# When the hidden product of a shared expert frees its banks, and where its steps stand among the routing

## What is computed

```python
    def swiglu(x):
        g = x[..., ::2]
        l = x[..., 1::2]
        g = jnp.minimum(g, LIMIT)
        l = jnp.clip(l, -LIMIT, LIMIT)
        return g * jax.nn.sigmoid(ALPHA * g) * (l + 1.0)
    xt = x.reshape(-1, d)
    scores = jax.nn.softmax(xt @ gate_w.T, axis=-1)
    _, idx = jax.lax.top_k(scores + gate_b, TOPK)
    ...
    h = swiglu((xt @ ew1 + eb1) * (xt @ ew3 + eb3))
    return (acc + ce[:, None] * (h @ ew2 + eb2), None)
    ...
    shared = swiglu((xt @ sw1 + sb1) * (xt @ sw3 + sb3)) @ sw2 + sb2
    return (routed + shared).reshape(b, s, d)
```

## Time and profile before

| | |
|---|---|
| time, median of 3 runs | 969.93 us (966.49 to 972.44) |
| time of the profiled execution | 972.44 us |
| its span | 970.7 us |
| PE busy | 889.3 us (92%) |
| DVE busy | 644.4 us (66%) |
| ACT busy | 529.9 us (55%) |
| POOL busy | 387.0 us (40%) |

### The profile page before, as it was taken

The page is one execution under the profiler, slowest core; times in us unless marked ns, Lnnn a source line. Parts: engine busy times, 40 slices in busy tenths (PEclk is TensorE's granted clock), DMA queues, the critical chain, the costliest instruction groups (busy, mean ns, idle before and its releaser), DMA issues.

```text
span 970.7 us, 15074 instructions
## 1 busy us (share of the span) xinstructions
PE 889.3 (92%) x4286; PEld 620.1 (64%) x4287; DVE 644.4 (66%) x1309; ACT 529.9 (55%) x843; POOL 387.0 (40%) x321
## 2 busy tenths in 40 slices
PE   8977667998999999999989999989999999999991
PEld 4633445554455555555447788878888888888881
DVE  4776997884565565574389678865666656566666
ACT  2525876536566657657653633424666666566650
POOL 2113441544477566567513554622222223122210
PEclk8977999999999999999999999999999999999996
DMA  9300000003775776785592500049531199416305
GB/s 304 97 0 0 1 0 1 0 1 107 287 279 201 305 275 233 276 339 207 231 349 86 217 1 1 6 182 422 226 128 32 48 334 348 190 59 268 104 28 174
DMA packets 49876, 154.05 MB, mean 159 GB/s; under 512 B 6234, under 2 KB 24406, under 8 KB 44204
## 3 DMA queue, kind: packets, MB, share of 16 engines
q1 hardware_dynamic: 46092, 144.25, 39.5%
q0 software_dynamic: 3744, 9.31, 3.0%
HBM read 97.85 MB, written 56.62 MB: 159 GB/s over the span
## 4 chain that ended last, share of the span: by engine, by line
PE 63%; DVE 18%; issue 5%; DMA 5%; ACT 4%; POOL 3%; SPq 1%; DVEq 0%; ACTq 0%; POOLq 0%
PE banks L1020 11%; PE banks L1269 6%; PE banks L1271 6%; PE banks L1270 6%; PE banks L989 3%; PE banks L1012 3%; DMA aux<-moe_x,small 3%; PE banks L1013 3%; PE banks L929 2%; DVE small L1889 2%; PE banks L1294 2%; DVE wexp L1902 2%; PE banks L1296 2%; PE banks L1295 2%; PE banks L1282 1%
## 5 line engine op out<-in xcount | busy, mean ns | idle before, releaser
L1020 PE MATMUL banks<-wexp 128*65 128x512 f32 (+1 forms) x288 | 149.2, 599 | 3.2 <-ACT wexp L1557 3.1
L658 POOL TENSOR_TENSOR cv_hl<-wexp,cv_hl 128x1024 fp32r<-128x1024 f32 x45 | 108.5, 2417 | 54.8 <-ACT cv_hl L1534 54.3
L1269 PE MATMUL banks<-ring,x_hi 128*128 x312 | 128.3, 411 | 0.0
L1271 PE MATMUL banks<-ring,x_lo 128*128 x312 | 122.7, 393 | 0.0
L1270 PE MATMUL banks<-ring,x_hi 128*128 x312 | 122.6, 393 | 0.0
L1557 ACT ACTIVATE wexp<-banks 128x512 f32<-128x512 f32 x128 | 76.3, 598 | 76.4 <-PE banks L1013 76.3
L2008 DVE TENSOR_REDUCE small<-banks 128x1 bf16<-128x1101 f32 x64 | 83.7, 1307 | 38.3 <-PE banks L989 38.3
L1689 ACT ACTIVATE banks<-wexp 128x1024 f32 x72 | 73.4, 1020 | 47.7 <-DVE aux L2357 47.7
L1672 ACT ACTIVATE aux<-banks 128x512 f32<-128x512 f32 x78 | 46.6, 597 | 64.4 <-PE banks L1271 48.3
L1012 PE MATMUL banks<-q_hi,k_hl 128*128 128x512 f32 x144 | 75.4, 523 | 1.7 <-ACT q_lo L1525 1.0
L726 POOL DMA_INDIRECT moe_y<-aux,small x20 | 20.6, 1030 | 118.2 <-DVE aux L2367 118.2
(11 more groups left out here) (356 smaller groups left out, 2213.0 us busy)
## 6 DMA issues: line engine op xcount, KB each, us to landing
wsplit<-cv_hl SPq DMA_DIRECT2D x45, 1024.0 KB, 8.0
ring<-wsplit SPq DMA_DIRECT2D x32, 1280.0 KB
wexp<-in_L_ffn_w SPq DMA_DIRECT2D x40, 512.0 KB, 6.0
wexp<-in_expert_biases SPq DMA_DIRECT2D x8, 1152.0 KB, 6.5
ring<-wsplit SPq DMA_DIRECT2D x4, 1024.0 KB, 8.5
wexp<-moe_y SPq DMA_DIRECT2D x8, 512.0 KB, 5.9
wexp<-in_L_ffn_sw SPq DMA_DIRECT2D x5, 512.0 KB, 9.1
x_sb<-in_x SPq DMA_DIRECT2D x4, 512.0 KB, 7.9
```

Source lines behind the costliest of these rows:

```text
L658: g.tensor_tensor(sides(hl[:, PIECE:2 * PIECE]), raw, sides(hl[:, 0:PIECE]).bitcast(f32), ALU.subtract).then_inc(s['cv_lo'], 1)
L1020: mm(pb[5 + half][0:DA, :], vh[b][0:w, c, :], pT[q % 3][0:w, :], start=c == 0, stop=c == len(KTILES) - 1).then_inc(s['a_pv'], 1)
L1269: mm(o[:], x_hi[u][:, kc, :], hi, start=kc == 0 and not primed, stop=False, skip_group_check=primed)
L1271: last = mm(o[:], x_lo[u][:, kc, :], hi, start=False, stop=primed and kc == KC - 1, skip_group_check=primed)
```

## The change

Four things are changed, all in the stage of the shared expert. The semaphore `h_up`, which counted all halves of the blocks, is now two, `h_w1` and `h_w3`. The semaphore `h_read` is gone: PE and ACT wait for the clamps (`h_gate`, `h_line`) where they waited for the products, and `line_sh` waits for its clamp before it raises `h_line` by an instruction of its own. On ACT, the steps around turns 1 to 4 stand in another order. On DVE, `gate_sh(2)`, `line_sh(4)` and `slot_experts()` have moved.

```diff
@@ up(ci, side), on PE
                 if ci > 0:
-                    pe.wait_ge(s['h_read'], 2 * ci - 1 + side)
+                    pe.wait_ge(s['h_line' if side else 'h_gate'], ci)
...
-                    last.then_inc(s['h_up'], 1)
+                    last.then_inc(s['h_w3' if j else 'h_w1'], 1)
@@ lifted_sh(ci, side), on ACT
-                act.wait_ge(s['h_up'], 4 * ci + 2 * side + 1)
+                act.wait_ge(s['h_w3'], 2 * ci + side + 1)
                 if ci > 0:
-                    act.wait_ge(s['h_read'], 2 * ci - 1 + side)
+                    act.wait_ge(s['h_line' if side else 'h_gate'], ci)
@@ the turns of the shared expert, on ACT
                 lifted_sh(ci, 0)
                 if ci > 0:
                     plus_one(ci - 1)
-                    if ci == 2:
-                        tokens_hi(4)
-                        tokens_hi(5)
                     hidden_hi(ci - 1)
-                if ci in (1, 3):
-                    logits_kept(ci)
+                if ci == 2:
+                    tokens_hi(4)
+                    tokens_hi(5)
                 if ci == 4:
-                    lifted_sh(ci, 1)
                     act.wait_ge(s['r_e'], 1)
                     a(score[:], score[:], ACT.Exp).then_inc(s['r_exp'], 1)
                     ready(ACT.Sigmoid)
                 chance(ci)
-                if ci != 4:
-                    lifted_sh(ci, 1)
+                if ci in (1, 3):
+                    logits_kept(ci)
+                lifted_sh(ci, 1)
@@ gate_sh(ci), on DVE
-                ve.wait_ge(s['h_up'], 4 * ci + 2)
+                ve.wait_ge(s['h_w1'], 2 * ci + 1)
...
-                v.scalar_tensor_tensor(gate, pb[UP_BANK[0][0]][:], bsh[:, 0, ci % IC, 0:1], lift[0], ALU.add, ALU.mult).then_inc(s['h_read'], 1)
-                ve.wait_ge(s['h_read'], 2 * ci + 1)
+                link(v.scalar_tensor_tensor(gate, pb[UP_BANK[0][0]][:], bsh[:, 0, ci % IC, 0:1], lift[0], ALU.add, ALU.mult))
                 v.tensor_scalar(gate, gate, LIMIT, None, ALU.min).then_inc(s['h_gate'], 1)
@@ line_sh(ci), on DVE
-                ve.wait_ge(s['h_up'], 4 * ci + 4)
+                ve.wait_ge(s['h_w1'], 2 * ci + 2)
...
-                v.scalar_tensor_tensor(line, pb[UP_BANK[1][0]][:], bsh[:, 0, ci % IC, 1:2], lift[1], ALU.add, ALU.mult).then_inc(s['h_read'], 1)
-                ve.wait_ge(s['h_read'], 2 * ci + 2)
-                v.tensor_scalar(line, line, LIMIT, -LIMIT, ALU.min, ALU.max).then_inc(s['h_line'], 1)
+                link(v.scalar_tensor_tensor(line, pb[UP_BANK[1][0]][:], bsh[:, 0, ci % IC, 1:2], lift[1], ALU.add, ALU.mult))
+                link(v.tensor_scalar(line, line, LIMIT, -LIMIT, ALU.min, ALU.max))
+                ve.sem_inc(s['h_line'], 1)
@@ the routing with the turns between, on DVE
+            gate_sh(2)
             tokens_low(4)
             tokens_low(5)
-            gate_sh(2)
             line_sh(2)
...
             gate_sh(4)
-            line_sh(4)
 
             ve.wait_ge(s['r_exp'], 1)
...
+            line_sh(4)
             link(v.tensor_tensor(bg1, theirs, mine, ALU.is_gt))
             gate_sh(5)
...
             gate_sh(15)
+            slot_experts()
             line_sh(15)
-            slot_experts()
             slots()
```

More of the change, by code:

```diff
@@ L335, in program @@
             r_x r_xT r_xhi r_xlo r_ghl r_lT r_lTs r_lTt r_e r_exp r_sel r_pos_full r_slot r_hot r_index r_meta r_bias bd_out ld_bias_f ld_bias_b r_hot_sh r_table r_start
-            h_up h_lift h_read h_gate h_line h_sig h_sg h_fP h_plus h_hi h_loP y_full y_add
+            h_w1 h_w3 h_lift h_gate h_line h_sig h_sg h_fP h_plus h_hi h_loP y_full y_add
             xst0 xst1 f_add ld_sh ld_sh2
```

## The result

| | before | changed |
|---|---|---|
| median, 9 runs each | 968.07 us (963.54 to 972.44) | 975.24 us (973.07 to 979.44) |
| ratio of the times, 95% interval | 1 | 1.0083 (1.0059 to 1.0106) |
| profiled execution: time, span, granted clock | 972.44, 970.7, 0.965 | 979.64, 977.9, 0.967 |
| product of gate_sh(0) to start of down(3) on PE | 514.04 to 634.48: 120.44 us | 513.03 to 642.54: 129.51 us |

The changed kernel is 0.8% slower, some 8 us. The last line of the table is the yardstick of all that follows: from the first operation of gate_sh(0) on DVE to the first matmul of down(3) on PE. The stage grew by 9.07 us.

What follows compares the result with a forecast made beforehand. PE bounds the shared-expert stage, DVE close behind. Terms 1.8 + 2.3 + 0.6 + 0.6 + 0.9 + 0.1 + 0.4 sum to 6.7 us on the median 969.93, giving 976.6 us; forecast range 4 to 10.5 us slower.

Steps and rivals of the forecast that it cites:

- the signs named for them: Changed profile: PE waits at up(5,1) and tokens_T(6), clamp and increment waits 5 us or more, clock dip, down(3) near 641.
- Release and increment at up(9,1) and up(11,1): PE already waits at these blocks and pays for clamp and signal: 0.6 us each, between 0.4 and 1.3 if POOL holds.
- Place 1: At tokens_T(6): gate_sh(2) ahead of tokens_low(4) and (5) on DVE delays PE by 1.8 us, bounds 1.1 and 1.9.
- (a): Rival: clock lost at up(5,1) and tokens_T(6), POOL holds clamps and slot_experts; 12.6 us, 982.5 us, chance 0.2.
- The cover that I named for the copy of the logits: Turns 1 and 3: copy's delay of under 1 us covered by the wait at tokens_T(6); 0.8 us if uncovered.
- Place 2: Turn 4, PE at up(5,1): lift behind the exponential, line_sh(4) behind the softmax sum; 2.3 us, range 1.7 to 2.7.
- 0.4 for the clock: One more clock fall, behind the new wait of about 2.4 us at up(5,1): 0.4 us, bounds 0 and 1.6.
- Turns 11 to 14: Round over all engines: later line_sh signal adds 0.1 to 0.2 us in five rounds; 0.9 us, between 0.3 and 1.9.
- slot_experts: Moved ahead of line_sh(15), its three operations fill DVE's idle 1.34 us: 0.1 us, up to 1.3 if POOL holds the last.
- (b): Rival: changes covered, wait at down(3) shrinks below what brings the clock down; time stays 970 to 973 us, chance 0.2.
- (c): Rival: exponential and routing 0.7 us earlier, line_sh(4) signals before 549.75, so faster than before, 966.2 us; chance 0.07.

Runs made afterwards that it cites:

- e5: Kernel before with only gate_sh(2) moved ahead of tokens_low(4) and (5) on DVE; executed once, stage 123.54 us against 120.44.
- e6: Kernel before with only ACT's order in turns 1 to 3 changed (hidden_hi(1) earlier, logits copies behind the sigmoid); executed once, stage 121.60 us against 120.44.
- e9: Kernel before with only the wait and separate increment in line_sh, banks still released by the products; ratio 1.0027, stage +2.10 us.
- e7: Kernel before with only the bank release moved behind the clamps, h_line raised by the clamp itself; ratio 1.0002, stage +1.91 us.
- e4: Kernel before with only slot_experts moved ahead of line_sh(15); ratio 1.0020, stage +0.98 us.
- e8: Kernel before with turn 15 shortened: ACT lifts side 1 ahead of the sigmoid, hidden product is one DVE operation; ratio 0.9952, stage -2.06 us.
- e11: e8 plus turn 4's sigmoid ahead of lift and exponential, line_sh(8) inside places(), line_sh(10) ahead of tiles_of_places(0); ratio to kernel before 0.9938, 961.42 us.
- e1: Kernel before with the release behind the clamps and the separate increment of h_line, all orders kept; ratio 1.0047, stage +4.31 us.
- e2: Kernel before with all moved orders on ACT and DVE, semaphores and releases as before; ratio 1.0062, stage +6.34 us.
- e10: Changed kernel with turn 15 shortened as in e8 and slot_experts back behind line_sh(15); ratio to kernel before 1.0074, stage 126.78 us.
- e3: Kernel before with only turn 4 changed: ACT lifts side 1 behind the exponential, line_sh(4) behind the softmax; ratio 1.0029, stage +2.34 us.

## Why the prediction was right, and where its terms were off

The forecast was 6.7 us more, the ratio gives 8 (5.7 to 10.3), the stage 9.07. The waits came at the places forecast, and the signs named for them came too: 6.8 us of waits for the clamps and the increment (5 or more were forecast) and a dip of the clock behind up(5,1). Two sizes were off, and one size was right for another reason than the one given. Term by term, forecast and measured in the stage:

- Release and increment at up(9,1) and up(11,1): 0.6 each; measured 0.5 each.
- Place 1, tokens_T(6): 1.8 with bounds 1.1 and 1.9; measured 3.0. **Mis-sized.** The wait came as forecast, 1.6 us longer (2.03 against 0.40), and the held clamp is part of it (1.12 for 0.43). What was not in the sum is the clock behind this wait: I had its loss only in the rival (a), and in the forecast only one fall, at up(5,1). From up(2,1) to up(3,1) the shift grows from 0.1 to 3.0 us, 1.3 more than the wait, with a granted clock of 0.50 at 534. By e5 the move of gate_sh(2) alone does all of it. The cover that I named for the copy of the logits did hold in the whole, by e5 and e6; without it the copy costs 0.72 at up(2,0), where I had put 0.8, and with hidden_hi(1) 1.07.
- Place 2, up(5,1): 2.3 and 0.4 for the clock; measured 2.5 at up(5,1), and 2.85 with what up(5,1) loses through the clock and up(6,0), up(6,1) get back through waits that vanish. The wait was forecast at 2.4 and is 2.32.
- Turns 11 to 14: 0.9; measured 1.1. **The size was right, the mechanism only in part.** I had 0.1 to 0.2 us in each of five rounds, by the later signal. On DVE the shift of the changed kernel is 6.4 us at line_sh(11), 7.7 at gate_sh(12) and 8.0 at gate_sh(15): nearly all of it comes at once, where the operation of 128x624 behind line_sh(11) is held (1.46 for 0.37). That it is the increment which brings this about is shown by e9 (0.65, 1.94 and 2.06) against e7 without it (1.39, 1.38 and 1.68). That the sum came near 0.9 is luck.
- slot_experts: 0.1, with 1.3 if POOL holds the last operation; measured 1.26 in the whole up to the start of line_sh(15), 1.25 in e4. **The wrong end of the bounds.** The upper one was worked out rightly. For the lower one I took about 0.2 us for the third operation, which the earlier trace rows do not show. The trace of the kernel before has it held as well, in its old place (the row below the list). I did not look at what else happens in the gap of 1.34 us. Behind POOL's operation of turn 14, which holds the clamp of gate_sh(15), POOL issues a transfer and then does its product, and that product starts 1.2 us after the clamp's end in the changed kernel (634.55 to 635.74) as in e4 (628.42 to 629.62). That is where the third operation stands, in all three profiles with this order. It was no matter of chance.
- Left over: 0.2 us come back at the end, since the clamp of line_sh(15) takes 0.43 us and no longer 0.67.

```profile
631.28 1.17 DVE L2267 TENSOR_SCALAR wexp<-wexp 128x39 f32<-128x39 f32 x1
```

By the measurement of the Trainium skill, page VectorE: DVE Perf Modes, section The DRAIN you can't avoid, that a semaphore behind each copy costs nothing extra, my sum would have been 0.6 us smaller. What e9 measured here, a wait and an increment of its own in each of the 16 line_sh, is not free: +2.10 us in the stage, more than half of it by way of the held operation.

The Trainium skill, page SBUF — State Buffer, section Who interferes with whom, says that a reduction does not contend with GpSimd and that a tensor_scalar in a two-port mode does. The trace agrees: TENSOR_REDUCE took 0.48 us in both orders, the TENSOR_SCALAR behind it 1.61 in the changed kernel. But I took from it that only the third operation can be held, and that is too narrow. In the trace of the kernel before a TENSOR_TENSOR of 128x128, which takes 0.29 us at 588.13, took 1.27 at 585.06, where POOL's operation of 584.83 was under way. The first operation of slot_experts took 0.48 us while POOL was at the issue of the transfer and not at a product.

The rivals. (a), all holds at once, needed 12.6 us. Its parts at tokens_T(6) and in slot_experts came, those at up(9,1) and up(11,1) did not: there the clamps took 0.43 us (at 585.17 and 603.71). (b), covered: it needed the wait at down(3) to shrink below the length that brings the clock down. It did not shrink, 2.72 against 2.61, because slot_experts lengthens the same chain (3.57 alone); with the releases alone it did, to 1.75 and 1.69. (c), faster: it needed a signal of line_sh(4) in time, and that comes 2.3 us after PE is ready, as forecast; only e8 and e11, which shorten what PE waits for, are faster.

The forecast of 976.6 lies closer to 975.24 than its terms deserve. They were 2.4 us short of the stage and 1.3 short of the ratio's 8 us, and the median that I added them to (969.93, of three runs) lay 1.9 us above that of nine.

## What to carry to other kernels

Where two engines are both near full, an order that moves an operation ahead of one that a third engine waits for can be paid twice, once as the wait and once more through the clock that falls behind it. Here it fell behind all eight new waits of 1.8 to 2.5 us at tokens_T(6) and up(5,1), so count both. Where DVE and POOL hold each other, a delay of 0.2 us can cost more than 1, because it puts an operation behind the start of one on the other engine: compare the starts, and not only the lengths. A small operation put into a gap is not free either if the other engine starts there on an event that hangs on the same one. And measure such a change on a stretch between two events of the program, not on the whole time: here the stretch repeated to 0.06 us and the whole to several.

## What the runs showed of the hardware

**The clock behind a wait.** Whether TensorE's clock falls behind a wait of 1.5 to 2.7 us is not settled by the wait's length. The 1.5 us at L1034 were followed by a fall in seven profiles of fourteen, above. At down(3), the first 10 us from its start: before (wait 2.61), e1 (1.75), e5 (2.64), e7 (1.69) and e9 (2.95):

```profile
634.48:644.48 10.00, 10.00 (x63) 9.23 (x64) 5.96 (x28) 0.38 (x1) 2.05 (x2) 0.83 0.17 42
```

```profile
634.81:644.81 10.00, 10.00 (x63) 9.27 (x64) 5.96 (x28) 0.38 (x1) 2.06 (x2) 0.83 0.19 49
```

```profile
633.21:643.21 10.00, 10.00 (x71) 8.83 (x72) 5.86 (x28) 0.47 (x2) 2.05 (x2) 1.00 0.27 83
```

```profile
631.35:641.35 10.00, 10.00 (x71) 8.85 (x72) 5.87 (x28) 0.49 (x2) 2.05 (x2) 1.00 0.26 79
```

```profile
634.37:644.37 10.00, 10.00 (x58) 9.60 (x59) 5.79 (x28) 0.39 (x1) 2.04 (x2) 0.70 0.09 27
```

e1 and e7 wait almost the same and differ in the clock; e5 waits as long as before and keeps it. It did not fall behind 1.05 us at down(3) of e8, 1.35 at up(13,0) of the changed kernel and 1.37 at up(6,0) of e1 and e7. At tokens_T(6) (changed, e2, e5, e10: 1.99 to 2.54 us) and at up(5,1) (changed, e2, e3, e10: 1.80 to 2.32) it fell each time, with 0.57 to 0.66 granted in the next 4 us. In the 10 us shown a fall costs 8 matmuls of 71 before and in e1, about 1.1 us, and 13 in e9, about 1.8. What decides it stays open. It can make a part of the spread of the times.

**What a wait on DVE costs.** A clamp of 0.43 us with nothing held behind it: the next operation starts 0.34 after the clamp does. With a wait and a separate increment, in the changed kernel:

```profile
517.11 0.43 DVE L2117 TENSOR_SCALAR aux<-aux 128x512 f32<-128x512 f32 x1
517.69 0.64 DVE L1764 BATCH_NORM_AGGREGATE small<-small 128x2 f32<-128x6 f32 x8 [0.15 <-DVE aux L2117]
```

0.58 after, so 0.24 us more for each line_sh where nothing else intervenes; 16 of them are 3.8 us on DVE, most of which falls where DVE has time. The 2.1 us that came through to down(3) in e9 are 0.6 up to turn 3 and 1.5 from turn 11 on, where the held operation stands.

**How long POOL holds a clamp.** In the trace before, the clamps of 128x512 that start while one of POOL's operations is under way end 0.28 or 0.29 us after it, whenever that is later than their own 0.43 us: 20 of the 32 clamps of the stage. The one at 518.12, which starts 0.25 us ahead of POOL's, takes 0.43.
